# A graph convolution on one core: plain destination matrices from GpSimd, every second weighted one from VectorE

## What is computed

```python
def _L2_gnn_ref(x, weight, bias, edge_index, edge_vals):
    support = x @ weight
    dst, src = (edge_index[0], edge_index[1])
    msgs = support[src] * edge_vals[:, None]
    out = jax.ops.segment_sum(msgs, dst, num_segments=x.shape[0])
    return out + bias

x = x + _L2_gnn_ref(_layernorm(x, axis=-1), L2_gnn_weight, L2_gnn_bias, edge_index, edge_weight)
```

## Time and profile before

| | |
|---|---|
| median of 3 runs | 1982.47 us (1979.96 to 1986.04) |
| the profiled execution's own time | 1988.3 us |
| its span (first to last instruction) | 1986.6 us |
| mean granted TensorE clock | 0.977 |
| PE busy | 94% of the span |
| DVE, ACT, POOL busy | 48%, 25%, 16% |

### The profile page before, as it was taken

One profiled execution on the slowest core, in us unless ns is written; L12 is line 12 of the kernel. 1 busy time (PEld: TensorE's weight loads), 2 busy tenths in 40 slices (PEclk: granted clock), 3 DMA queues, 4 the chain that ended last, 5 costly groups with the idle time before them and its releaser, 6 DMA issues. The chain is left out here.

```text
span 1986.6 us, 27055 instructions
## 1 busy us (share of the span) xinstructions
PE 1866.3 (94%) x8836; PEld 1038.3 (52%) x8836; DVE 955.5 (48%) x2860; ACT 505.0 (25%) x1388; POOL 320.6 (16%) x343
## 2 busy tenths in 40 slices
PE   7999998999899999999998799879789999999999
PEld 4464557677544434533453333335435444578876
DVE  9662643000179887997799611156532223331102
ACT  1171641111134352234224412127110000010000
POOL 0000001334327404720571000000000000010001
PEclk9999999999999999999999899989899999999999
DMA  4102019998277406730678189944352232149884
GB/s 169 59 17 75 1 47 392 398 339 318 39 260 225 131 1 199 209 89 2 181 208 292 63 302 387 386 137 152 128 191 74 90 144 108 40 153 390 327 324 153
DMA packets 180664, 357.47 MB, mean 180 GB/s; under 512 B 29072, under 2 KB 38560, under 8 KB 180524
## 3 DMA queue, kind: packets, MB, share of 16 engines
q1 hardware_dynamic: 157548, 285.42, 40.0%
q0 software_dynamic: 22976, 70.23, 12.1%
HBM read 333.91 MB, written 21.69 MB: 179 GB/s over the span
## 5 line engine op out<-in xcount | busy, mean ns | idle before, releaser
L1256 PEld LDWEIGHTS ps<-tokT,w 128*128 128x128 f32 x2304 | 259.8, 192 | 11.4 <-issue 6.7
L1256 PE MATMUL ps<-tokT,w 128*128 128x128 f32 x2304 | 260.6, 275 | 3.8 <-DVE tokT L1406 2.4
L1729 POOL DMA_INDIRECT w<-xl_d,src_i x216 | 215.0, 995 | 290.5 <-DMA xl_d<-XL 222.7
L1825 PE MATMUL ps<-XP,wide 128*128 (+1 forms) x456 | 185.2, 507 | 0.0
L1830 PE MATMUL ps<-w,ident 128*128 128x512 f32 x270 | 140.7, 602 | 8.7 <-DMA w<-xl_d,src_i 8.5
L1825 PEld LDWEIGHTS ps<-XP,wide 128*128 128x128 f32 x456 | 81.4, 188 | 72.7 <-issue 67.4
L1940 ACT ACTIVATE wide<-oht 128x128 fp32r<-128x128 bf16 x228 | 68.1, 308 | 198.4 <-PE ps L1830 178.5
L1275 PE MATMUL ps<-w,O 128*128 128x512 f32 x256 | 112.5, 597 | 0.0
L1491 POOL DMA_INDIRECT spread_d<-N,slot x12 | 11.8, 981 | 583.0 <-DVE slot L1363 580.0
L2102 DVE SCALAR_TENSOR_TENSOR w<-ps,w 128x512 f32<-128x512 f32 x144 | 98.1, 681 | 5.2 <-PE ps L1830 5.0
L1425 DVE TENSOR_TENSOR hT<-act,ps 128x512 f32<-128x512 f32 x20 | 13.7, 687 | 178.0 <-ACT act L1311 178.0
(11 more groups left out here) (534 smaller groups left out, 3029.6 us busy)
## 6 DMA issues: line engine op xcount, KB each, us to landing
w<-L_ffn_W SPq DMA_DIRECT2D x16, 2048.0 KB, 14.1
w<-L_ffn_W SPq DMA_DIRECT2D x8, 4096.0 KB, 18.0
w<-fc1T SPq DMA_DIRECT2D x32, 1024.0 KB, 14.4
w<-fc2T SPq DMA_DIRECT2D x30, 1024.0 KB, 14.3
w<-L_ffn_w_down SPq DMA_DIRECT2D x10, 2048.0 KB, 14.9
w<-L_ffn_w_gate SPq DMA_DIRECT2D x20, 1024.0 KB, 9.5
w<-L_ffn_w_up SPq DMA_DIRECT2D x20, 1024.0 KB, 12.2
w<-L_ffn_w SPq DMA_DIRECT2D x8, 2048.0 KB, 13.4
```

Of the source, the lines that this page charges most:

```text
L1256: m = pe.matmul(k.ps[:, 1 + (q * ins + i) % 4, s * P:(s + 1) * P], self.W1[u][i][:, f, (q * T + s) * P:(q * T + s + 1) * P], self.tokT[:, ...
L1729: gp.indirect_dma_start(self.G[:, u, :], None, k.xl_d, bass.IndirectOffsetOnAxis(ap=k.src_i[:, i:i + 1].bitcast(U32), axis=0)).then_inc(k. ...
L1825: m = pe.matmul(bank, self.wide[:, i % DEEP, :], self.XP[:, q].rearrange("p t n -> p (t n)")[:, bass.ds(at, D)], start=False, stop=(q == 1 ...
```

## The change

In words: POOL gets a program in this stage that makes all 72 plain matrices `od`, each behind the same `conv_added` wait, and signals `placed`. DVE no longer makes `od`. For every odd tile DVE makes, behind `os_`, the first weighted matrix `dw[u][0]` straight from the ramp, with a comparison and a multiplication by the weight in one instruction. ACT makes the second weighted matrix of the odd tiles from `od`, and both of the even tiles. PE's program is the same.

```diff
+        def by_vector(i):
+            return i % 2
+
         with nc.Block() as block:
+            @block.gpsimd
+            def _(gp):
+                for i in range(EB):
+                    if i >= AHEAD:
+                        gp.wait_ge(k.conv_added.sem, k.conv_added.at(i - AHEAD + 1))
+                    gp.tensor_scalar(od[i % AHEAD][:], k.ramp[:, 0:P], k.dst_f[:, T + i:T + i + 1], None, ALU.is_equal
+                                     ).then_inc(k.placed.sem, 1)
+
@@ VectorE, place(i)
                     edge = slice(T + i, T + i + 1)
-                    v.tensor_scalar(od[u][:], k.ramp[:, 0:P], k.dst_f[:, edge], None, ALU.is_equal
-                                    ).then_inc(k.placed.sem, 1)
-                    v.tensor_scalar(os_[u][:], k.ramp[:], k.src_f[:, edge], None, ALU.is_equal
-                                    ).then_inc(k.conv_ready.sem, 1)
+                    m = v.tensor_scalar(os_[u][:], k.ramp[:], k.src_f[:, edge], None, ALU.is_equal)
+                    if by_vector(i):
+                        m = v.tensor_scalar(dw[u][0][:], k.ramp[:, 0:P], k.dst_f[:, edge], wf[0][:, i:i + 1],
+                                            ALU.is_equal, ALU.mult)
+                    m.then_inc(k.conv_ready.sem, 1)
@@ ScalarE, weigh(i)
                     a.wait_ge(k.placed.sem, k.placed.at(i + 1))
-                    for q in range(2):
+                    for q in range(by_vector(i), 2):
                         m = a.activation(dw[u][q][:], od[u][:], ACT.Copy, scale=wf[q][:, i:i + 1])
                     m.then_inc(k.weighed.sem, 1)
```

## The result

| | before | after |
|---|---|---|
| median | 1983.61 us (8 runs, 1979.9 to 1987.4) | 1992.39 us (8 runs, 1990.2 to 1996.4) |
| ratio | | 1.0048, 95% interval 1.0034 to 1.0063 |
| span of the profiled execution | 1986.6 us | 1993.5 us |
| first norm instruction to the copy of the banks | 1315.44 to 1378.72: 63.3 us | 1315.15 to 1387.24: 72.1 us |
| copy of the banks to the end | 607.8 us | 606.2 us |

The profiled executions differ by up to 5 us in front of the stage and by as much behind it, so in what follows one number stands for a kernel's stage: the time from DVE's first norm instruction to ACT's first copy of the banks, read from two rows of the timeline of one execution. It grew by 8.8 us, and so did the median. Nothing behind it grew.

What follows compares the result with a forecast made beforehand. DVE, slowed by POOL's turns, would bound the stage: 25.2 + 2.4 = 27.6 us for 48 tiles, copy at 1374.0, gain 4.7 us, so 1982.5 - 4.7 = 1977.8 us; 8-in-10 range 1974.5 to 1987.0.

Steps and rivals of the forecast that it cites:

- rival (c): POOL, waiting on each turn, bounds the tiles: slower than before from 0.667 us an `od`, 1991.3 us at 0.85; chance 0.12.
- POOL's own pace: POOL's `od` in turns with DVE: one per 0.43 us possible, 0.5 us available, so not the bound.
- The reading of before: Tiles before the change: ACT sets the pace at 0.587 us, DVE is 4% behind, PE could go at 0.457.
- The ceiling of 6.5 us: Most the stage can gain: without waits PE would let the copy start at 1372.2 instead of 1378.7.
- DVE's part: DVE drops `od` (0.16 us) and makes odd tiles' weighted matrix (0.25); a pair of tiles costs 1.05 us alone.
- c for two turns: Time one POOL `od` adds to DVE by holding SBUF: 0.035 to 0.065 us, taken as 0.05.
- rival (b): POOL's long hold makes DVE slower than ACT was; loss from a 0.25 us hold, 1984.8 us at 0.3; chance 0.24.
- The sharing itself: DVE and POOL take turns on SBUF without overlap; a 128-column POOL operation holds DVE 0.14 to 0.17 us.
- The part behind the copy: Stages after ACT's copy of the banks: nothing changes length, the later stages shift as a whole.
- The price of the comparison: POOL's 128-column `od`, priced from `ident` and `before` 0.25 us apart and `zrow`, four times as wide, 0.51.
- Who waits in a turn: DVE's `os` waits for POOL's hold: a turn of both takes 0.43 to 0.46 us where DVE alone needs 0.40.
- these additions as hidden: DVE's bias addition, 2.49 us behind its last tile, ends after the copy starts, yet PE has DVE's bank in time.

Runs made afterwards that it cites:

- run with DVE quiet: The changed kernel with DVE's one-hots left out from tile 12 on; stage 61.3 us, 2.0 us shorter than before.
- the summing form: The changed kernel with the 512-wide one-hot `os` also summing its row into a spare column; stage 71.1 us, one run 1989.65 us.
- POOL's matrices alone: The changed kernel, but DVE makes only the 512-wide matrices and ACT weighs both of every tile; ratio 1.0039, stage 71.7 us.

## Why the prediction was wrong

Forecast 1977.8 us, 4.7 us faster; measured 1992.39, 8.8 us slower, outside the range to 1987.0. The time was that of rival (c), POOL's own pace, which had a chance of 0.12 and 1991.3 us at 0.85 us a matrix; measured were 0.829.

What held:

- The reading of before. ACT at 0.587 us a tile was the bound, DVE close behind, PE at 0.457 free. The ceiling of 6.5 us was met within 0.2 us by the two kernels that leave DVE and POOL short (6.3 and 6.5).
- DVE's part. The new matrix costs 0.26 us (taken 0.25), a pair of tiles without `od` 1.08 beside POOL in most of the stream, at times up to 1.24 (forecast, with c for two turns: 1.12 to 1.18; at 1.08 there was only one turn in it). DVE was slowed, but it was not what the end waited for: rival (b) did not happen.
- The sharing itself, read from the first 4 us. Where DVE streams, POOL's matrices end 0.14 us behind the end of a DVE instruction, as `before` did in the earlier trace rows.
- The part behind the copy: 607.8 us became 606.2.

What failed is the step "POOL's own pace: ... in turns with DVE one `od` per 0.43 us is possible, and it has 0.5 us". Two terms in it were wrong. The run with DVE quiet takes the second away and shows the first; the summing form takes the second away while DVE streams:

- *The price of the comparison.* It was taken from a select and a memset (0.25 us apart). Those keep their price in this stage; the comparison takes 0.58 us from start to start with DVE quiet. That alone is over the 0.5 us that the same step names as the limit, and with it alone the gain was 2.0 us (stage 61.3 us).
- *Who waits in a turn.* The rows of the start showed each engine waiting once for the other. I put the cost on DVE, c for each `od`, and gave POOL a turn behind each DVE instruction. In the stream DVE loses little (`os` 0.47 and 0.51 us of duration), and POOL loses most: 1.08 us for 0.58. That it arrives only after its own preparation, and then waits through the instruction under way and often through the next, is a reading that fits these rows; no run shows it. Over tiles 24 to 71 POOL's own pace is 48 x 0.577 = 27.7 us of the 39.77, and the sharing is the other 12.1. Of these, 1.4 us fell beside the bias additions, where three matrices took 1.10, 1.30 and 0.78 us from start to start; the prediction had counted these additions as hidden.

The second term is what turned the sign. With the first alone put right, the sum of rival (c) gives 1345.2 + 48 x 0.58 + 0.3 + 1.2 = 1374.5, still a gain of 4.2 us and close to the forecast. The stage with DVE quiet is 2.0 us shorter than before and with DVE streaming 8.8 longer: the 10.8 us between them come from the sharing with the one-hots. The Trainium skill's page "GPSIMD Engine Reference", section "Performance versus the Vector engine", which was weighed in the prediction, gives 2.6 cycles of 1.2 GHz for an element as its upper figure, by which 128 columns take 0.28 us, an estimate from that page. Measured were 0.34 for the columns (128 x 2.6 ns) and 0.24 more for the instruction. I set the page aside for rows of another operation; it pointed the right way and not far enough.

## What to carry to other kernels

A price belongs to an operation and not to an engine: before work goes to an engine that has never run that instruction in the trace, take the pace that it must keep and ask by what factor the nearest row could be off; here it was off by two, and that alone took the helper over its limit. When a helper engine takes one step of every tile it must keep up with every tile; give it a share of the tiles that it can finish in its worst pace, and choose the step that relieves the bound directly. And where two engines share a path, look which of them loses: a turn-taking pair in a short stretch does not say who waits when one of them streams. Look at the end of the stage too: one last matrix of the helper beside four additions cost 2 us.

## What the runs showed of the hardware that I had not expected

- GpSimd's comparison of 128 columns against a pointer takes 0.58 us from start to start, from f16 and from f32 alike, and 0.61 against a constant; 64 columns take 0.41. Its copy, select and memset of 128 columns last half as long or less (0.30, 0.29, 0.21 us against 0.60).
- Beside DVE's fast `tensor_scalar` stream a GpSimd comparison of 0.58 us takes up to 1.08 from start to start (0.93 beside `os` alone, 1.20 in the kernel that gives POOL two matrices in four tiles), and the one of 0.78 takes 1.0 to 2.4, depending on the order of DVE's instructions. DVE loses 0.03 us for a turn with the change and 0.13 in the kernel with POOL's matrices alone. Beside DVE additions with two SBUF inputs an instruction of 0.24 us took 2.6, and one of 0.58 took 3.6. Beside DVE's summing form GpSimd loses nothing.
- In the changed kernel the granted TensorE clock fell to 0.52 between 1359 and 1362 us, that is to the lower of its levels, behind 6 us in which PE had been busy 4.3; it was back at 1.00 afterwards. Before the change PE had no gaps there and the clock stayed at 1.00. It did not set the end of the stage: POOL's row has no gap in these 3 us either.
